# A float32r attention and quantised-FFN layer: right-side buffers moved by 160 bytes, DRAM tensors in blocks, the first loads on two queues

## What is computed

```python
x = x + attn(layernorm(x), Wq, Wkv, Wo)            # 32 query heads of 32, one shared key/value head, ALiBi bias, causal
x = x + layernorm(x) @ dequant(qweight).T + bias   # 1024 x 1024 weight of 6-bit codes, scale and zero point per row
```

## Time and profile before

| | us |
|---|---|
| median of 3 runs | 821.62 (820.59 to 821.73) |
| the profiled execution | 822.31 |
| its span, first to last instruction | 820.5 |
| PE busy | 806.4 (98%) |
| DVE / ACT / POOL busy | 594.7 / 372.5 / 429.4 |

### The profile page before, as it was taken

One profiled execution on the slowest core, in us unless ns is written; L12 is line 12 of the kernel. 1 busy time (PEld: TensorE's weight loads), 2 busy tenths in 40 slices (PEclk: granted clock), 3 DMA queues, 4 the chain that ended last, 5 costly groups with the idle time before them and its releaser, 6 DMA issues.

```text
span 820.5 us, 13647 instructions
## 1 busy us (share of the span) xinstructions
PE 806.4 (98%) x4618; PEld 583.2 (71%) x4618; DVE 594.7 (72%) x1589; ACT 372.5 (45%) x730; POOL 429.4 (52%) x313
## 2 busy tenths in 40 slices
PE   7999999999999999999999999999999999999997
PEld 5777878888665655556555555688887888888886
DVE  3877554577878889988888896255647779684877
ACT  1755536232466677676666665221401231051322
POOL 1000000000299998899889988522746298363566
PEclk9999999999999999999999999999999999999999
DMA  8867687467566655676566655462064613500012
GB/s 313 315 199 209 229 256 256 154 177 223 152 140 150 152 132 146 146 160 143 134 146 172 156 122 172 151 180 89 1 224 136 198 60 111 194 28 1 38 65 103
DMA packets 71390, 125.85 MB, mean 153 GB/s; under 512 B 7460, under 2 KB 16708, under 8 KB 71240
## 3 DMA queue, kind: packets, MB, share of 16 engines
q1 hardware_dynamic: 71312, 124.97, 52.5%
q10 hardware_dynamic: 8, 0.01, 0.0%
HBM read 85.61 MB, written 38.94 MB: 152 GB/s over the span
## 4 chain that ended last, share of the span: by engine, by line
PE 77%; DMA 7%; DVE 6%; issue 4%; ACT 4%; POOL 1%; SPq 0%; DVEq 0%; POOLq 0%; ACTq 0%
PE p_s L870 11%; PE p_st L899 9%; PE p_o L910 9%; PE p_s L978 5%; PE p_s L980 5%; PE p_s L979 5%; PE p_o L923 5%; PE p_o L809 4%; DMA inv_b<-inv_d 3%; PE p_s L809 2%; PE p_st L978 2%; PE p_st L980 2%; PE p_st L979 2%; PE p_s L1003 2%; PE p_s L1002 2%
## 5 line engine op out<-in xcount | busy, mean ns | idle before, releaser
L1452 DVE CUSTOM_DVE_ANT_0 spill<-p_s,mask 128x128 bf16<-128x128 f32 (+3 forms) x512 | 219.6, 483 | 38.3 <-PE p_s L870 37.6
L1169 ACT ACTIVATE pt<-p_st 128x512 f32<-128x512 f32 (+1 forms) x352 | 178.2, 562 | 101.1 <-PE p_st L899 100.9
L635 POOL TENSOR_SCALAR_AFFINE_SELECT pt<-pt 128x512 f32<-128x512 f32 x128 | 87.5, 696 | 238.7 <-ACT pt L1169 238.7
L870 PE MATMUL p_s<-kst,xt 98*128 98x128 f32 (+3 forms) x512 | 151.1, 343 | 0.9 <-DVE mx L1452 0.7
L899 PE MATMUL p_st<-xt,kst 100*128 100x512 f32 (+1 forms) x352 | 129.4, 387 | 0.7 <-DMA xt<-ml 0.3
L870 PEld LDWEIGHTS p_s<-kst,xt 98*128 98x128 f32 x512 | 91.4, 189 | 52.7 <-DVE mx L1452 42.7
L642 POOL TENSOR_TENSOR pt<-pt 128x1536 f32<-128x1536 f32 x32 | 111.8, 3492 | 2.7
L910 PE MATMUL p_o<-pt,vst 128*32 128x512 f32 (+3 forms) x1024 | 82.4, 439 | 0.0
L648 POOL TENSOR_TENSOR pt<-pt 128x1024 f32<-128x1024 f32 x32 | 76.7, 2396 | 0.0
L899 PEld LDWEIGHTS p_st<-xt,kst 100*128 100x128 f32 x352 | 64.5, 190 | 14.1 <-issue 5.6
L809 PE MATMUL p_o<-xt,wqh 128*128 128x512 f32 x136 | 53.1, 400 | 0.8 <-DVE xt L1603 0.8
(11 more groups left out here) (205 smaller groups left out, 1648.0 us busy)
## 6 DMA issues: line engine op xcount, KB each, us to landing
xt<-qh_d SPq DMA_DIRECT2D x64, 256.0 KB
xs<-in_x_t_dram SPq DMA_DIRECT2D x32, 256.0 KB, 6.2
qh_d<-qh SPq DMA_DIRECT2D x32, 256.0 KB, 3.2
ql_d<-ql SPq DMA_DIRECT2D x32, 256.0 KB, 4.1
xt<-ql_d SPq DMA_DIRECT2D x32, 256.0 KB
o_d<-o_st SPq DMA_DIRECT2D x32, 256.0 KB, 2.3
ob<-o_d SPq DMA_DIRECT2D x32, 256.0 KB, 5.5
xin<-in_x_dram SPq DMA_DIRECT2D x14, 512.0 KB, 7.8
```

The costliest lines, as they stand in the source:

```text
L635: pool.affine_select(out=own, in_=own, compare_op=ALU.is_ge, fill=0.0, base=0, pattern=[[0, 4], [1, P]], channel_multiplier=-1).then_inc(c ...
L870: pe.matmul(scores_of(n), qst[s % 4][0:R_MAX, j, qb * P:(qb + 1) * P], kst[0:R_MAX, b * S:b * S + keys], start=True, stop=True).then_inc(s ...
L1169: act.activation(pt[s % 2][:, j:j + heads, PT_AT[kb]:PT_AT[kb] + KB_LEN[kb]], p_st[:, place(k) % 3, 0:heads * KB_LEN[kb]].rearrange("p (j ...
L1452: dve.tensor_tensor_reduce(spill[:, SPILL_AT[qb]:SPILL_AT[qb] + keys], scores_of(n), mask[:, S - keys:S], 1.0, LOWEST, ALU.add, ALU.max, m ...
```

## The change

Five edits:

1. A dummy buffer of 160 bytes is the first on the right side. All right buffers then start at 320 modulo 512, like the left ones.
2. `x_t`, `wq`, `wo`, the output, `qh_d`, `ql_d` and `o_d` are laid out in DRAM as blocks of [128, 512], each contiguous (256 KB). The number, sizes and SBUF sides of the DMAs stay; `qweight_t`, x in rows and `wi_d` stay as they were.
3. SP issues the loads of x chunks 0, 2, 4, 6, and ACT those of 1, 3, 5, 7, then `raw_kv`, then the small position table that it issued before.
4. The mean is made of four pairs: the fourth sum goes to `rstd_b[:, 0, :]`, which is free then. Two matmuls in place of four passes on single chunks become one pair (two passes). The dummy matmuls go from ten to six.
5. ACT's first activation is a one-element square root, ahead of its first copy.

```diff
         sb = tensors(ctx, "right")
+
+        sb("to_512_bytes", [P, 40])
         woh, wol = sb("woh", [P, CK, D], F32R), sb("wol", [P, CK, D], F32R)
...
-        pair = (qt[:, 0, :], qt[:, 1, :], mean_b[:, :])
+        pair = (qt[:, 0, :], qt[:, 1, :], mean_b[:, :], rstd_b[:, 0, :])
...
-                sp.dma_start(xs[:, c, :], xt_v[:, c, b * S:(b + 1) * S]).then_inc(xs_in[c], 16)
+                sp.dma_start(xs[:, c, :], x_t[b, c]).then_inc(xs_in[c], 16)
...
-                    sp.dma_start(qh_d[rows, cols], qh[:, m % 2, :].bitcast(F32)).then_inc(q_out[m % 2], 16)
+                    sp.dma_start(qh_d[b, m], qh[:, m % 2, :].bitcast(F32)).then_inc(q_out[m % 2], 16)
...
-            for c in range(CK):
+            for c in range(0, CK, 2):
                 load_xs(0, c)
-            sp.dma_start(raw_kv[:, :, :], wkv.rearrange("p (c n) -> p c n", c=CK)).then_inc(kv_in, 16)
             for u in range(CK):
                 load_wq(u)
...
-                for _ in range(10):
+                for _ in range(6):
                     pe.matmul(p_mean[:, 0:P], share[:, :], mx[0][:, :], start=True, stop=True)
-                for i in range(3):
+                for i in range(4):
                     pe.wait_ge(pair_done, i + 1)
-                    pe.matmul(p_mean, share[:, :], pair[i], start=(i == 0), stop=False)
-                for c in (6, 7):
-                    pe.wait_ge(xs_in[c], 16)
-                    last = pe.matmul(p_mean, share[:, :], xs[:, c, :], start=False, stop=(c == 7))
+                    last = pe.matmul(p_mean, share[:, :], pair[i], start=(i == 0), stop=(i == 3))
...
+            for c in range(1, CK, 2):
+                act.dma_start(xs[:, c, :], x_t[0, c]).then_inc(xs_in[c], 16)
+            act.dma_start(raw_kv[:, :, :], wkv.rearrange("p (c n) -> p c n", c=CK)).then_inc(kv_in, 16)
             act.dma_start(kt[R_BIAS:R_END, :], kpos).then_inc(kpos_in, 16)
+            act.wait_ge(consts, 5)
+
+            act.activation(mv[:, 0, 3:4], eps[:, 0:1], ACT.Sqrt).then_inc(table_in, 1)
             act.wait_ge(kv_in, 16)
             act.copy(wkv2[:, :, 0:64], raw_kv[:, :, :]).then_inc(kv_hi, 1)
-            act.wait_ge(consts, 5)
...
-    qh_d = nc.dram_tensor("qh_d", [D, ROWS], F32, kind="Internal").ap()
+    qh_d = nc.dram_tensor("qh_d", [B, CK, P, S], F32, kind="Internal").ap()
```

More of the change, by code:

```diff
@@ L252, in layer @@
         x_rows = x.rearrange("b s d -> (b s) d")
-        xt_v = x_t.rearrange("(c p) n -> p c n", p=P)
-        wq_v = wq.rearrange("(c p) n -> p c n", p=P)
+        xt_v = x_t.rearrange("b c p q -> b p c q")
         qw_v = qweight_t.rearrange("(a p j) n -> a j p n", a=2, j=3)
@@ L363, in load_wq @@
                 at_least(sp, raw_in[c], 16 * half)
-                sp.dma_start(raw[:, u, :], wq_v[:, c, half * S:(half + 1) * S]).then_inc(raw_in[c], 16)
+                sp.dma_start(raw[:, u, :], wq[half, c]).then_inc(raw_in[c], 16)
             def load_x(T):
@@ L415, in project @@
                     n = CK * b + m
-                    rows, cols = slice(m * P, (m + 1) * P), slice(b * S, (b + 1) * S)
                     sp.wait_ge(qh_done, n + 1)
-                    sp.dma_start(qh_d[rows, cols], qh[:, m % 2, :].bitcast(F32)).then_inc(q_out[m % 2], 16)
+                    sp.dma_start(qh_d[b, m], qh[:, m % 2, :].bitcast(F32)).then_inc(q_out[m % 2], 16)
                     sp.wait_ge(ql_done, n + 1)
-                    sp.dma_start(ql_d[rows, cols], ql[:, m % 2, :].bitcast(F32)).then_inc(q_out[m % 2], 16)
+                    sp.dma_start(ql_d[b, m], ql[:, m % 2, :].bitcast(F32)).then_inc(q_out[m % 2], 16)
                     if more and m == TURN_M[b] - 1:
@@ L442, in load_q @@
                     sp.wait_ge(ext_out, 16)
-                rows, cols = slice(P * g, P * g + P), slice(b * S, (b + 1) * S)
                 for r, src in enumerate((qh_d, ql_d, qh_d)):
                     sp.dma_start(qst[s % 4][32 * r:32 * r + 32, :, :].bitcast(F32),
-                                 src[rows, cols].rearrange("(j d) q -> d j q", j=4)).then_inc(q_in[s % 4], 16)
+                                 src[b, g].rearrange("(j d) q -> d j q", j=4)).then_inc(q_in[s % 4], 16)
                 sp.dma_start(qst[s % 4][R_BIAS:R_MAX, :, :].bitcast(F32),
@@ L458, in store_o @@
                 sp.wait_ge(o_taken, s + 1)
-                sp.dma_start(o_d[P * g:P * g + P, b * S:(b + 1) * S], o_st[:, :]).then_inc(o_out, 16)
+                sp.dma_start(o_d[b, g], o_st[:, :]).then_inc(o_out, 16)
             def load_wo(h):
                 at_least(sp, wo_lo, h - 3)
-                sp.dma_start(wo_half(ob, h), wo_v[:, h // 2, S * (h % 2):S * (h % 2) + S]).then_inc(wo_in[h % 4], 16)
+                sp.dma_start(wo_half(ob, h), wo[h // 2, h % 2]).then_inc(wo_in[h % 4], 16)
             def attend(s):
@@ L508, in load_x2 @@
                 of = slice(4 * half, 4 * half + 4)
-                sp.dma_start(x2[t % 2][:, of, :], xt_v[:, of, t * S:(t + 1) * S]).then_inc(x2_in[t % 2][half], 16)
+                sp.dma_start(x2[t % 2][:, of, :], xt_v[t][:, of, :]).then_inc(x2_in[t % 2][half], 16)
             def load_o(k):
@@ L522, in load_o @@
                     at_least(sp, o_lo, k - 3)
-                sp.dma_start(ob[:, k % 4, :], o_d[P * g:P * g + P, b * S:(b + 1) * S]).then_inc(o_in[k % 4], 16)
+                sp.dma_start(ob[:, k % 4, :], o_d[b, g]).then_inc(o_in[k % 4], 16)
             def load_inv(k):
@@ L1677, in build @@
 def build(nc, x, x_t, wq, wkv, wo, qweight_t, rows, kpos, slopes, out_t):
-    qh_d = nc.dram_tensor("qh_d", [D, ROWS], F32, kind="Internal").ap()
-    ql_d = nc.dram_tensor("ql_d", [D, ROWS], F32, kind="Internal").ap()
+    qh_d = nc.dram_tensor("qh_d", [B, CK, P, S], F32, kind="Internal").ap()
+    ql_d = nc.dram_tensor("ql_d", [B, CK, P, S], F32, kind="Internal").ap()
     ext_d = nc.dram_tensor("ext_d", [2, HEADS * S], F32, kind="Internal").ap()
@@ L1682, in build @@
     inv_d = nc.dram_tensor("inv_d", [B, P, S], F32, kind="Internal").ap()
[L1683 removed]
+    o_d = nc.dram_tensor("o_d", [B, CK, P, S], F32, kind="Internal").ap()
     st_d = nc.dram_tensor("st_d", [B, 2 * S], F32, kind="Internal").ap()
@@ L1717 @@
     given = {
-        "x": x, "x_t": x.reshape(ROWS, D).T, "wq": np.asarray(L0_attn_Wq)[order],
+        "x": x, "x_t": x.reshape(B, S, CK, P).transpose(0, 2, 3, 1),
+        "wq": np.asarray(L0_attn_Wq)[order].reshape(CK, P, 2, S).transpose(2, 0, 1, 3),
         "wkv": np.asarray(L0_attn_Wkv)[order].reshape(CK, P, 2 * HD).transpose(1, 0, 2).reshape(P, CK * 2 * HD),
-        "wo": np.asarray(L0_attn_Wo)[:, order], "qweight_t": np.asarray(L0_ffn_qweight)[order].T,
+        "wo": np.asarray(L0_attn_Wo)[:, order].reshape(CK, P, 2, S).transpose(0, 2, 1, 3), "qweight_t": np.asarray(L0_ffn_qweight)[order].T,
         "rows": np.concatenate([np.asarray(v).reshape(D)[order].reshape(CK, P).T for v in (
@@ L1729 @@
         args.append(nc.dram_tensor(f"in_{name}_dram", a.shape, mybir.dt.from_np(a.dtype), kind="ExternalInput").ap())
-    out_t = nc.dram_tensor("out_dram", (D, ROWS), F32, kind="ExternalOutput").ap()
+    out_t = nc.dram_tensor("out_dram", (B, CK, P, S), F32, kind="ExternalOutput").ap()
     build(nc, *args, out_t)
     r = _run(nc, [arrays], core_ids=[0])
-    return np.ascontiguousarray(np.asarray(r.results[0]["out_dram"])[np.argsort(order)].T).reshape(B, S, D)
+    out = np.asarray(r.results[0]["out_dram"]).transpose(0, 3, 1, 2).reshape(B, S, D)
+    return np.ascontiguousarray(out[:, :, np.argsort(order)])
```

3 lines of the change are left out of this document (1 added, 2 removed).

## The result

The changed kernel takes 815.71 us, median of 4 runs (815.34 to 816.08), against 821.54 for the kernel before in the same comparison: ratio 0.9931, 95% interval 0.9914 to 0.9949, a gain of 5.8 us. The profiled execution takes 815.39 us with a span of 813.7. The forecast was 817.6, a gain of 4.05; the range and the sign hold, the sum is 1.8 us short, and part of that is a step that was wrong (the second queue, which was put at nothing).

What follows compares the result with a forecast made beforehand. PE, in flight for 98% of the span, was taken to bound the kernel. Terms 1.65 + 2.1 + 0.1 + 0.2 = 4.05 us, taken from the median 821.62, gave 817.6 us; range 814.9 to 820.8.

Steps and rivals of the forecast that it cites:

- Edit 1: 1.65 forecast: Mixed-side matmuls in o1, f3 and the sums fall to 227 ns: 1.65 us gained, bounds 0 and 2.3.
- The rival that the phase doesn't matter: Another difference of o1 and f3 slows their matmuls, so the filler gains nothing: 819.3 us, chance 0.05.
- The two large terms: Faster matmuls: 1.2 us in o1 (192 matmuls), 0.35 us in f3 before the sum of squares (48 matmuls).
- `share_r` x `pr`: The sums' 24 matmuls, weights left and data right, get faster: 0.15 us, 0.1 counted.
- The tail of f3: After the sum of squares DVE sets the end; the remaining 80 matmuls' possible 0.6 us counted as nothing.
- Edits 2 and 3: 2.1 forecast: First x loads: the 8 KB pitch slows the stream; blocks gain 2.1 us, 70% of at most 3.0.
- The second queue brings nothing by rows: Start loads: issuing a chunk (0.43 us) is faster than its transfer (0.66 us), so a second queue gains 0.
- Edit 4: 0.1 forecast: Four pairs end the mean 0.5 us sooner at PE's start; 0.1 us counted.
- The absorption by row tile 3: The wait for row tile 3, landed at 30.7 us, swallows the mean's gain; afterwards only the stream's gain lasts.
- Clock and six dummies: At the start, six dummies keep PE busy until about 7.3 us; counted as 0 us.
- the 6 of the rival: With six dummies the clock is still 1.2 GHz when projections begin, adding 6 us: 823.6 us, chance 0.04.
- Edit 2 elsewhere: Queries, outputs and `wo` in blocks: 0.2 us gained, bounds 1.5 us faster and 0.5 slower.

Runs made afterwards that it cites:

- experiment 1: The kernel before with only the 160-byte filler added: 819.32 us, ratio 0.9976.
- experiment 10: The changed kernel without the 160-byte filler: 818.33 us, ratio 0.9968 against the kernel before.
- experiment 3: The kernel before with only the loads split over two queues (x chunks on SP and ACT, `raw_kv` on ACT), old pitch: 820.03 us.
- experiment 6: The changed kernel with all x chunks and `raw_kv` issued from SP again: 817.26 us.
- experiments 5 to 7: The changed kernel with one edit taken back each: old mean with ten dummies 817.34 us; all x chunks and `raw_kv` from SP 817.26; old DRAM layout 817.23.
- experiments 2 and 6: The kernel before with only the DRAM blocks, 819.45 us; and the changed kernel with all x chunks and `raw_kv` from SP, 817.26 us.
- experiment 5: The changed kernel with the old mean (three pairs, two single chunks, ten dummies): 817.34 us.
- experiment 11: The changed kernel with one dummy matmul in place of six: 816.11 us.

## Why the prediction came out as it did

**Edit 1: 1.65 forecast, 2.0 measured alone and 2.6 when taken out.** The mechanism holds: nothing else changed in experiment 1, and both stages fell to the predicted 227 ns. The rival that the phase doesn't matter is refuted, and with it the 0 that the prediction drew from the Trainium skill's "SBUF — State Buffer", section "Who interferes with whom". That section says that PE never waits on anyone; it speaks of other engines and is silent on PE's own two operands, whose place costs 3% here. The traces don't speak for another engine either: through all of f3 in before, whatever DVE and POOL do meanwhile, the distances repeat one cycle of eight (230, 232, 238, 237, 231, 234, 235, 233 ns).

The two large terms came out: o1 gave 1.3 us (1.2 in the sum), and f3 from its first matmul to the end of the span 0.4 (0.35), in experiment 1 and between 10 and after alike. The mis-sized term is the third, 0.1 us for `share_r` x `pr`. In before it isn't these matmuls alone that are slow: after each sum and each change of stage the next ten or so matmuls stand 229 to 236 ns apart, though their own operands start alike. With the 160 bytes such places have 226 to 228, and the matched "f" stages go from 227.5 to 226.8 ns in the mean. Between experiment 10 and after this makes f1, o3 and f2 0.12 to 0.13 us shorter each. The 1.1 us between f0 and f3 there are these three and 0.76 us in o2, of which 0.7 is the stop for `o_a`; that comes and goes, so I don't credit it to the edit.

**The tail of f3: right.** PE's last matmul ends 4.9 us before the end of the span, 4.4 in before and 4.3 in experiment 10. The chain of work of the kernel after at its end, against the earlier trace rows: DVE evicts and adds once in 1.70 us.

```profile
807.85 0.75 DVE ob L1589
808.60 0.03 issue
...
809.55 0.75 DVE ob L1589
810.30 0.03 issue
...
810.39 0.75 DVE x_odd L1595
```

Between experiment 10 and after PE ends 3.3 us apart and the span 2.7: only part of f3 is gained, as the sum said. The 0.6 us between the two is what the sum put at nothing, the 80 matmuls behind the sum of squares.

**Edits 2 and 3: 2.1 forecast; blocks near it, second queue wrong.** "The second queue brings nothing by rows" failed. I had argued that issuing (0.43 us a chunk) is faster than transfer (0.66), so that the queue can't be the limit. Experiment 3 has 394 GB/s at the old pitch, and experiment 6 with blocks but one queue has 326. Here the Trainium skill's "DMA: Bandwidth & Descriptors", section "Issuing engines are not separate DMA queues", was no help either: it grants a second queue only issue time, and the last chunk, issued 2.4 us earlier than in before, landed at 9.28 with a rate a third higher (394 against 258 to 302). The DMA share was a row that I passed over: 0.88 in before and 1.05 with two queues, where a stream at full rate has 1.05. Engines stood partly idle although loads were queued; that speaks against slow transfers as the only cause.

Blocks work too, alone by 1.85 us where I had 2.1 for the stream and 0.2 elsewhere. But the working behind the 2.1 was only partly right, and that the sizes are so near is partly luck. I took the pitch as the cause of the whole mean rate; with one queue the rate from 4 to 9 us is 258 to 302 GB/s at the pitch and 313 and 326 in blocks, somewhat over a third of the way to 394. And PE starts only 0.6 to 1.05 us earlier by blocks alone (12.76 against 13.35 to 13.81); another 0.5 us comes between 33 and 121 us, from the edit's other parts or from the stream, which no run tells apart. Either cure takes most of the loss of the last landing (9.55 and 9.28 from 10.2 to 11.5), both together give 9.0, and the gains of the two hardly add up at PE's start: 13.35 to 13.8 without either, 12.76, 13.38, and 11.83 with both and the new mean.

What one queue lacks isn't settled. It loses its time among the first chunks, in either layout (experiments 5 to 7), and reaches full rate later. Single 2 KB transfers take up to 1.6 us at the start of before, but 0.84 in experiment 1 with the same pitch and queue, 0.9 with blocks on one queue (experiments 2 and 6), 0.6 at the old pitch on two (experiment 3), and 0.2 in after from 3.5 us on: so the pitch isn't all of it.

**Edit 4: 0.1 forecast, 0.6 or more measured.** From the last landing to the mean's end after takes 2.0 us, near the 1.8 of the prediction. What failed is the comparison: the mean was put against the kernel before, where the loads are late. Edits 2 and 3 changed the bound: with landings 2 us earlier the ten dummies and the single passes would be PE's limit (experiments 3 and 5), and then four fewer dummies count. My sum had the terms one by one, each against the kernel before; no run has this edit alone on it. The absorption by row tile 3 is there, but smaller than I said: experiment 11 shows the 0.8 us gone at 30 us, and 0.4 us of it back behind 32.7; experiment 5 has 0.6 us left at the attention. Its 1.6 us by medians I can't fully place.

**Clock and six dummies: right.** The granted clock is at 2.4 GHz from 7.7 us on, 4 us before the projections. Even with one dummy it is from 10.9 on, still before them, and the cost is 0.4 us, not the 6 of the rival. The Trainium skill, "TensorE: Matmul & The Clock Gate", section "What's actually happening", lists the two levels, 1.2 and 2.4 GHz. The traces agree: 0.85 and 0.43 us from pass to pass is a factor of two.

**Edit 5:** not tried alone. The table load that it saves, 1.28 us at 21.24 in before, is followed by 0.45 us of waiting on ACT; in after ACT waits 1.46 us there. I have no run that tells the edit from zero. **Edit 2 elsewhere:** forecast 0.2; in the traces PE gains 0.5 us between 33 and 121 us, the wait at `xt` low is 0.3 shorter, and the first stores of `ql_d` land 2.1 us after issue where one took 2.78.

**Sum.** Alone on the kernel before, edit 1 gives 2.0, blocks 1.85, queues 1.3, in all 5.15 of the 5.8 us; 0.65 is left for edits 4 and 5. The forecast has 1.65 + 2.1 + 0.2 + 0.1. Of the 1.8 us missing, 0.35 is edit 1, about 0.85 the second queue (3.15 for the stream, 0.2 of elsewhere included, against 2.3), and 0.55 the mean, which is what is left over and not a measurement. All three lie within what one comparison can tell or close to it, 0.8 us on each side. The terms aren't separate either: taken out of the changed kernel one by one, the 160 bytes, the mean, the second queue and the blocks cost 2.6, 1.6, 1.55 and 1.5 us, 7.3 in all, more than the 5.8 that they bring together.

## What to carry to other kernels

When stages with the same matmul have different distances, compare where weights and moving data start in SBUF: a filler of 160 bytes was worth 2 us of 820. A load stream below full rate with a DMA share under 1 wasn't at its limit here, whatever the mean rate suggested: look at each load's landing for the gap, and try a second issuing queue and contiguous blocks before you argue from issue time. And when one edit makes data earlier, go through the consumer's fixed work again (warm-up matmuls, single passes), because what was hidden behind the loads now sets the start.

## What the runs showed of the hardware

- A float32r matmul of 512 columns follows the last after 226.7 ns when weights and moving data start at the same place modulo 512 bytes, and after 233 to 234 ns when they are 128 or 160 bytes apart; 64 bytes apart gave 233.3 in one order of the sides and 228.9 in the other.
- The slowness outlasts its cause: after two mixed matmuls (the sums), or a change of both operands from one side to the other, some ten matched ones stand 229 to 236 ns apart before they fall back to 227, in kernels whose sides are 160 bytes apart.
- Eight loads of 256 KB in 2 KB pieces, from 4 to 9 us: 258 to 302 GB/s with an 8 KB pitch on one queue, 313 and 326 as blocks on one queue, 380 and 394 with the pitch on two, 375 to 399 as blocks on two. A second read of the same addresses was no faster (283). On one queue a gap of 1.6 to 2.75 us stands among the first five landings, and the last chunk comes at full rate.
- The start varies between executions by up to 1.25 us: four kernels with the same instructions up to there have their first projection matmul at 13.35 to 14.60 us.
- Warm-up matmuls delay real work when data come early: with ten until 7.4 us (experiment 3), a pair ready at 5.8 waited 1.6 us.
